# All eight cosine products of the rotary embedding on GpSimd, in a one-core vision transformer layer

## The chip, the core and the metric

The kernel runs on one core of one Trainium2 chip. The metric is the device time of one execution in microseconds (us). The core's engines are named as the profile names them: PE is TensorE (matmul; PEld its weight loads), DVE is VectorE, ACT is ScalarE, POOL is GpSimd, SP is SyncE, which here only starts transfers (DMA).

## What is computed

The input is 32 images of 256 x 256. Each goes through a wavelet tokenizer, then one transformer layer on 257 tokens (a class token and 256 rows) of width 256: a 16-head causal attention with rotary embedding, and a feed-forward part with quantised weights and activations. Cut to what matters here:

```
qkv = jnp.einsum('bsd,dhf->bshf', x, w_qkv) + b_qkv
q, k, v = jnp.split(qkv, 3, axis=-1)
q = q * cos + _rotate_half(q) * sin
k = k * cos + _rotate_half(k) * sin
scores = jnp.einsum('bhqd,bhkd->bhqk', q, k) / jnp.sqrt(jnp.float32(f)) + alibi, causal mask, softmax
h = h + einsum(attn, w_out) + b_out
h = h + ffn(layernorm(h))        # silu(gate) * up, then down; activations quantised row by row
```

## The kernel before, in words

The 32 images pass through a software pipeline of steps. A step `s` works on three images at once: part A (tokenizer and first layer norm) of image s+1, part B (the projections q, k, v and the rotary embedding) of image s, and parts C and E (attention and the feed-forward part) of image s-1. Five steps at the start and four at the end are written out; the 26 between are a loop of 13 passes over two steps. Each step has 16 slots, `k` = 0 to 15, and every engine walks the slots in the same order; what it does in a slot is fixed by tables (`QK_SLOT`, `V_SLOT`, `GU_SLOT` and others). An engine runs its own instructions strictly in order, and waits on semaphores for the others.

The rotary embedding is done in eight groups g = 0 to 7 of two 128-row blocks: groups 0 to 3 are q, groups 4 to 7 are k. They stand in slots 1, 2, 3, 4, 5, 7, 8, 9. For a group:

- PE computes the projection into `b_bank`; ACT copies it with its bias into `rq[:, g % 2]` (L501, semaphore `rq_ready`).
- SP copies `rq` to `rot[:, g % 2]` with the halves swapped, in four transfers (L392, `rot_done`). It waits for `qk_done` of group g-2, since `rot` has two halves.
- The cosine product `rq * cos` goes straight into `qt` or `kt`. It is on POOL (L475, `pcos_done`) for the groups of `COS_ON_POOL` and on DVE (L1175, `t1_done`) for the others. A q group is one instruction on 2 x 256 columns. A k group is two instructions on 2 x 128 columns, because the class token's column lies between them. The tiles `qt` and `kt` are called arena in the profile.
- POOL multiplies `rot` by the sine in place (L480, `t2_ready`) and adds it to the cosine product (L484, `qk_done`).

DVE does its cosine product in slot k of the group, POOL does all its work for the group one slot later. ACT may overwrite `rq[:, g % 2]` with group g+2 once the cosine product and the swap of group g are done (`wait_cos`). PE needs all eight groups (`qk_done`) in slot 14, for the scores of the image's first heads.

Other work that the prediction names. On DVE: `ttr` (L1055) moves scores out of PSUM with bias and row maximum; `pt_lo` (L1060, out ptr_l) makes the low half of the transposed probabilities, for which PE waits before `values`; `normalise` (L1079, out ao); the quantisation of the tokens in slot 5 (L1096 and what follows); `xn` (L1190, two instructions in slot 9), the first layer norm; `vl` (L1170), the low half of v, for which PE waits before the next v block. On POOL: the power for the second layer norm (L462, `rstd2`, in slot 5, ahead of group 3), the power for the first (L465, slot 7), and in slots 8 and 9 `hr` (L491) and `row_operators` (L446 to L455) between groups 5 and 6.

Of the kernel before, what the change touches and what calls it, by code (L numbers as in the profile page):

```python
# [40 lines left out]
WSCALE = 64.0  # L41
MAGIC = 1.5 * 2.0 ** 23
SLOTS = 16
COS_ON_POOL = [1, 3, 4, 6]
QK_GROUPS = 8


# [60 lines left out]
def vit_layer(nc, x, cls_tok, Wa, ba, Wd1, bd1, Wd2, bd2, Wd3, bd3, w_qkv, b_qkv, w_out, b_out,  # L108
              w_gate, w_up, w_down, c_cos, c_sin, c_rel, c_mask, c_row, c_avg, c_eye, out):
    with ExitStack() as ctx:  # L110
# [213 lines left out]
        def wait_cos(eng, b, g):  # L324

            on_pool = g % QK_GROUPS in COS_ON_POOL
            groups = [i for i in range(QK_GROUPS) if (i in COS_ON_POOL) == on_pool]
            done = len([i for i in groups if i <= g % QK_GROUPS]) + (len(groups) if g >= 0 else 0)
# [102 lines left out]
        def _(pool):  # L431
# [25 lines left out]
            def step(s, par):  # L457
                has_a, has_b, has_c, has_e = stages(s)
                for k in range(SLOTS):
# [8 lines left out]
                    if has_b and k - 1 in QK_SLOT:  # L468
                        g = QK_SLOT.index(k - 1)
                        if g in COS_ON_POOL:  # L470
                            pool.wait_ge(rq_ready, 8 * s + g + 1)
                            if g == COS_ON_POOL[0] and (not isinstance(s, int) or s > 1):
                                pool.wait_ge(t_done, 32 * (s - 1))
# [398 lines left out]
        def _(dve):  # L872
# [247 lines left out]
            def step(s, par):  # L1120
# [5 lines left out]
                for k in range(SLOTS):  # L1126
# [39 lines left out]
                    if has_b and k in V_SLOT:  # L1166
# [3 lines left out]
                        stt(vl[par][:, v // 2, cols], b_bank[:, :], 1.0 / WSCALE, vh[par][:, v // 2, cols], ALU.mult, ALU.subtract).then_inc(vl_done, 1)  # L1170
                    if has_b and k in QK_SLOT and QK_SLOT.index(k) not in COS_ON_POOL:
                        g = QK_SLOT.index(k)
# [98 lines left out]
```

## Time and profile before

| | before |
|---|---|
| median of 3 runs | 2415.41 us (2415.02 to 2421.36) |
| the profiled execution | 2422.74 us, span 2420.7 us |
| PE busy | 1851.4 us (76% of the span) |
| DVE busy | 1731.4 us (72%) |
| ACT busy | 1359.0 us (56%) |
| POOL busy | 1023.0 us (42%) |
| mean granted clock of PE | 0.933 of full speed |

Busy time is the sum over the whole span; no engine is busy throughout, since each waits for the others at fixed points of every step. A timeline row gives start and length in us, engine, line, what is written and read, the number of instructions, and in brackets the idle time before it and what ended that idle time.

### The profile page before, as it was taken

The numbers are of one execution on the slowest core, as the hardware profiler recorded it, in microseconds if no ns is written. First come the engines' busy times: TensorE is split into PE (matmuls) and PEld (weight loads), VectorE is DVE, ScalarE is ACT, GpSimd is POOL, SyncE is SP. The second block draws the span as 40 slices with busy tenths as digits, with TensorE's granted clock in tenths as the row PEclk, the third lists the DMA queues.
The fourth block names the chain that finished last, engine by engine and source line by source line (L and its number), as shares of the span: only waits on it lengthen the run. The fifth ranks groups of instructions, "written<-read, shape, count | busy, mean of one in ns | idle before, by whom it ended". The sixth has DMA issues, their size and how long they took to land.

```text
span 2420.7 us, 54955 instructions
## 1 busy us (share of the span) xinstructions
PE 1851.4 (76%) x16742; PEld 1334.8 (55%) x16742; DVE 1731.4 (72%) x5024; ACT 1359.0 (56%) x3841; POOL 1023.0 (42%) x1098
## 2 busy tenths in 40 slices
PE   2667878777787887777878787778778787887775
PEld 2644555555555655555556555555555555555543
DVE  2536778778777677777767776877767677777775
ACT  0125666666656565655656656665655565666653
POOL 0136445444555344445544443455534344554400
PEclk6769999999999999999999999999999999999986
DMA  7312111111111111111111111111111111111100
GB/s 180 127 35 53 40 43 49 42 42 40 42 48 49 46 41 44 42 38 40 49 50 48 39 45 40 40 39 48 49 46 41 40 42 36 47 49 45 45 10 9
DMA packets 98170, 114.79 MB, mean 47 GB/s; under 512 B 22722, under 2 KB 60067, under 8 KB 97571
## 3 DMA queue, kind: packets, MB, share of 16 engines
q1 hardware_dynamic: 97826, 110.61, 17.6%
q8 instruction: 167, 2.74, 0.5%
q14 instruction: 177, 1.44, 0.2%
HBM read 26.62 MB, written 8.42 MB: 14 GB/s over the span
## 4 chain that ended last, share of the span: by engine, by line
PE 35%; DVE 29%; issue 20%; ACT 9%; POOL 3%; SPq 2%; DVEq 1%; ACTq 0%; DMA 0%; POOLq 0%
PE bank L624 16%; PE bank L774 4%; DVE arena L1055 3%; DVE ptr_l L1060 3%; DVE arena L1207 3%; DVE es L1210 3%; DVE th L1203 3%; PE bank L858 3%; PE bank L714 2%; PE bank L712 2%; PE bank L726 2%; ACT arena L509 2%; DVE ao L1079 2%; PE bank L735 1%; PE bank L658 1%
## 5 line engine op out<-in xcount | busy, mean ns | idle before, releaser
L480 POOL TENSOR_TENSOR rot<-rot,sin 128x512 f32<-128x512 f32 x256 | 331.0, 1293 | 1072.4 <-DMA rot<-rq 1072.2
L509 ACT ACTIVATE arena<-arena,nm 128x129 f32<-128x129 f32 (+1 forms) x1024 | 458.5, 457 | 65.0 <-DVE nm L1055 65.0
L1055 DVE CUSTOM_DVE_ANT_0 arena<-bank,bias 128x129 f32<-128x129 f32 (+1 forms) x1024 | 304.9, 354 | 174.1 <-PE bank L714 164.5
L624 PE MATMUL bank<-xt_h,weights 128*128 128x256 f16 x2048 | 398.1, 282 | 20.1 <-ACT rq L501 17.6
L624 PE MATMUL bank<-arena,ptr_h 128*128 128x64 f16 x3072 | 211.1, 196 | 258.1 <-DVE ptr_l L1060 161.1
L514 ACT ACTIVATE ptr_h<-bank 128x384 f16<-128x384 f32 x512 | 249.9, 488 | 231.4 <-PE bank L726 231.3
L501 ACT ACTIVATE rq<-bank,bqk 128x256 f32<-128x256 f32 x512 | 213.8, 469 | 275.6 <-PE bank L624 270.9
L484 POOL TENSOR_TENSOR arena<-arena,rot 128x256 f32<-128x256 f32 (+1 forms) x384 | 344.4, 911 | 30.3 <-POOL rot L480 0.5
L624 PEld LDWEIGHTS bank<-arena,ptr_h 128*128 128x128 f16 x3072 | 182.1, 100 | 305.8 <-DVE ptr_l L1060 226.8
L1060 DVE TENSOR_TENSOR ptr_l<-bank,ptr_h 128x384 f16<-128x384 f32 x512 | 281.5, 550 | 53.8 <-ACT ptr_h L514 53.7
L624 PE MATMUL bank<-xt_l,weights 128*128 128x256 f16 x1024 | 288.5, 282 | 0.0
L726 PE MATMUL bank<-eye,arena 128*128 128x128 f32 x1536 | 267.3, 284 | 0.0
L624 PEld LDWEIGHTS bank<-xt_h,weights 128*128 128x128 f16 x2048 | 206.5, 101 | 88.9 <-issue 29.4
L726 PEld LDWEIGHTS bank<-eye,arena 128*128 128x128 f32 x1536 | 188.4, 146 | 65.6 <-issue 38.0
L1175 DVE TENSOR_TENSOR arena<-rq,cos 128x256 f32<-128x256 f32 (+1 forms) x192 | 132.0, 714 | 123.8 <-ACT rq L501 123.8
L624 PE MATMUL bank<-weights,xt_h 128*128 128x512 f16 x512 | 155.4, 385 | 71.1 <-DVE arena L1170 69.6
L509 ACT ACTIVATION_READ_ACCUMULATOR arena<-arena,nm 128x1 f32 x1024 | 204.7, 200 | 0.0
L624 PE MATMUL bank<-arena,ptr_l 128*128 128x64 f16 x1536 | 194.4, 196 | 0.0
L624 PE MATMUL bank<-weights,arena 128*128 128x256 f16 x1536 | 179.0, 273 | 2.8 <-DVE arena L1060 2.6
L475 POOL TENSOR_TENSOR arena<-rq,cos 128x256 f32<-128x256 f32 (+1 forms) x192 | 178.2, 942 | 0.0
L714 PE MATMUL bank<-arena 64*128 64x257 f32 x1024 | 161.1, 392 | 0.0
L624 PEld LDWEIGHTS bank<-weights,arena 128*128 128x128 f16 x1536 | 149.4, 98 | 20.7 <-DVE arena L1060 3.1
(187 smaller groups left out, 3562.1 us busy)
## 6 DMA issues: line engine op xcount, KB each, us to landing
rot<-rq SPq DMA_DIRECT2D x1024, 64.0 KB, 2.0
arena<-in_x SPq DMA_DIRECT2D x4, 2048.0 KB, 18.2
xin<-in_x SPq DMA_DIRECT2D x32, 256.0 KB, 2.7
hr<-hr SPq DMA_DIRECT2D x32, 256.0 KB, 2.4
out<-h SPq DMA_DIRECT2D x64, 128.0 KB, 1.7
arena<-in_L_attn_w_qkv SPq DMA_DIRECT2D x2, 1536.0 KB, 6.5
arena<-in_L_attn_w_out SPq DMA_DIRECT2D x1, 1024.0 KB, 10.1
arena<-in_L_ffn_w_gate SPq DMA_DIRECT2D x1, 1024.0 KB, 6.4
```

What stands on the lines that cost most here:

```text
L475: ins = pool.tensor_tensor(dst, rq[:, g % 2, :, cols], cos[:, cols].unsqueeze(1).broadcast_to([P, 2, cols.stop - cols.start]), ALU.mult)
L480: pool.tensor_tensor(r, r, sin[:, :].unsqueeze(1).broadcast_to([P, 2, SIDE]), ALU.mult).then_inc(t2_ready, 1)
L484: ins = pool.tensor_tensor(dst, dst, rot[:, g % 2, :, cols], ALU.add)
L501: return act.activation(dst, src, ACT.Identity, **kw)
L509: act.activation(cols, cols, ACT.Exp, bias=nm[:, t, h:h + 1], scale=-1.0, accum_out=rs[:, t, h:h + 1]).then_inc(e_done, 1)
L514: act.activation(dst, src, ACT.Copy).then_inc(hi_done, 1)
L624: ins = pe.matmul(dst, lhs[l], rhs[r], start=start and n == 0, stop=stop and n == len(parts) - 1)
L714: pe.matmul(bank[:, W0:SCOLS], qt[par][half, j, P:SIDE], kt[par][half, j, :], start=True, stop=True).then_inc(s_ready, 1)
L726: ins = pe.transpose(pt_bank[use % 2][:, n * P:(n + 1) * P], r[:, col:col + P], eye[:, :])
L1055: dve.tensor_tensor_reduce(r[:, cols], bank[:, cols], b, -1.0, 3.0e38, ALU.add, ALU.min, nm[:, t, h:h + 1]).then_inc(t_done, 1)
L1060: tt(dst, src, hi, ALU.subtract).then_inc(pt_free, 1)
L1175: ins = tt(dst, rq[:, g % 2, :, r], cos[:, r].unsqueeze(1).broadcast_to([P, 2, r.stop - r.start]), ALU.mult)
```

## The change

The table that names the groups whose cosine product is on POOL now holds all eight.

```diff
-COS_ON_POOL = [1, 3, 4, 6]
+COS_ON_POOL = list(range(8))
```

The code that reads the table stays as it is. DVE's branch is never taken, and `wait_cos` always waits on `pcos_done`. The wait on `t_done` that keeps POOL's first cosine product of an image from overwriting a `qt` still in use is now ahead of group 0 instead of group 1.

On DVE, in a written-out step, at the end of slot 8 and in slot 9 (`es` are scales of the quantisation, `ptr_l` the low probabilities, `xn` the first layer norm, `arena<-rq,cos` the cosine product):

```order
 L1117 TENSOR_SCALAR es<-es,wsc 128x1 [waits chain_e]
 L1118 TENSOR_SCALAR es<-es 128x1
-L1175 TENSOR_TENSOR arena<-rq,cos 128x2x128 [waits rq_ready]
-L1175 TENSOR_TENSOR arena<-rq,cos 128x2x128
 L1060 TENSOR_TENSOR ptr_l<-bank,ptr_h 128x384 [waits hi_done]
 L1190 TENSOR_SCALAR xn<-hh,mv,rstd 128x256 [waits rstd_ready]
```

Group 7's two instructions are gone from between the scales and the low probabilities; groups 0, 2 and 5 go in the same way from slots 1, 3 and 7.

On POOL, from the start of an image to the power of the second layer norm, before:

```order
L480 TENSOR_TENSOR rot<-rot,sin 128x512 [waits rot_done0]
L484 TENSOR_TENSOR arena<-arena,rot 128x512 [waits t2_ready,t1_done]
L475 TENSOR_TENSOR arena<-rq,cos 128x512 [waits t_done,rq_ready]
L480 TENSOR_TENSOR rot<-rot,sin 128x512 [waits rot_done1]
L484 TENSOR_TENSOR arena<-arena,rot 128x512 [waits t2_ready,pcos_done]
L480 TENSOR_TENSOR rot<-rot,sin 128x512 [waits rot_done0]
L484 TENSOR_TENSOR arena<-arena,rot 128x512 [waits t2_ready,t1_done]
L462 TENSOR_TENSOR rstd<-ve,negh 128x2 [waits var2_ready]
```

and the same place with the change:

```order
L475 TENSOR_TENSOR arena<-rq,cos 128x512 [waits t_done,rq_ready]
L480 TENSOR_TENSOR rot<-rot,sin 128x512 [waits rot_done0]
L484 TENSOR_TENSOR arena<-arena,rot 128x512 [waits t2_ready,pcos_done]
L475 TENSOR_TENSOR arena<-rq,cos 128x512 [waits rq_ready]
L480 TENSOR_TENSOR rot<-rot,sin 128x512 [waits rot_done1]
L484 TENSOR_TENSOR arena<-arena,rot 128x512 [waits t2_ready,pcos_done]
L475 TENSOR_TENSOR arena<-rq,cos 128x512 [waits rq_ready]
L480 TENSOR_TENSOR rot<-rot,sin 128x512 [waits rot_done0]
L484 TENSOR_TENSOR arena<-arena,rot 128x512 [waits t2_ready,pcos_done]
L462 TENSOR_TENSOR rstd<-ve,negh 128x2 [waits var2_ready]
```

A cosine product (L475) now stands ahead of the sine product of group 0, and another ahead of that of group 2. In the same way one of two instructions comes ahead of group 5 (after the power L465) and one ahead of group 7 (the last of the image).

## Rows read from the trace of the kernel before

**Rows 1.** PE's waits from 200 to 2300 us: total us, times, longest us

```profile
PE bank L624 <- DVE ptr_l L1060: 154.3, 92, 4.2
PE bank L624 <- DVE arena L1170: 63.0, 58, 1.8
```

**Rows 2.** Groups by line and shape, 500 to 2000 us: busy us, mean ns, idle before

```profile
L475 POOL TENSOR_TENSOR arena<-rq,cos 128x256 f32<-128x256 f32 x86 | 63.5, 759 | 0.0
L475 POOL TENSOR_TENSOR arena<-rq,cos 128x512 f32<-128x512 f32 x43 | 57.3, 1333 | 0.0
L1175 DVE TENSOR_TENSOR arena<-rq,cos 128x256 f32<-128x256 f32 x86 | 45.8, 573 | 41.0 <-ACT rq L501 41.0
L1175 DVE TENSOR_TENSOR arena<-rq,cos 128x512 f32<-128x512 f32 x44 | 45.7, 1038 | 34.4 <-ACT rq L501 34.4
```

**Rows 3.** Timeline of DVE around the cosine products of groups 0, 2 and 5

```profile
1016.50 0.68 DVE L1175 TENSOR_TENSOR arena<-rq,cos 128x512 f32<-128x512 f32 x1
...
1018.23 0.29 DVE L1055 CUSTOM_DVE_ANT_0 arena<-bank,bias 128x129 f32<-128x129 f32 x1 [0.58 <-PE bank L714]
...
1024.83 1.67 DVE L1175 TENSOR_TENSOR arena<-rq,cos 128x512 f32<-128x512 f32 x1 [1.01 <-ACT rq L501]
...
1028.70 0.29 DVE L1055 CUSTOM_DVE_ANT_0 arena<-bank,bias 128x129 f32<-128x129 f32 x1 [1.74 <-PE bank L714]
...
1044.91 0.76 DVE L1175 TENSOR_TENSOR arena<-rq,cos 128x256 f32<-128x256 f32 x2 [2.04 <-ACT rq L501]
...
1046.74 0.69 DVE L1203 SCALAR_TENSOR_TENSOR th<-th,bank 128x512 f32<-128x512 f32 x1 [0.60 <-ACT th L591]
```

**Rows 4.** Timeline of DVE at group 7, in two consecutive steps

```profile
1054.90 1.05 DVE L1175 TENSOR_TENSOR arena<-rq,cos 128x256 f32<-128x256 f32 x2
1055.87 0.55 DVE L1060 TENSOR_TENSOR ptr_l<-bank,ptr_h 128x384 f16<-128x384 f32 x1
1056.34 1.13 DVE L1190 TENSOR_SCALAR xn<-hh,mv,rstd 128x256 f32<-128x256 f32 x2
...
1127.06 1.83 DVE L1175 TENSOR_TENSOR arena<-rq,cos 128x256 f32<-128x256 f32 x2
```

**Rows 5.** Timeline of PE in the first of these steps, after group 7

```profile
1056.47 0.23 PE L624 MATMUL bank<-arena,ptr_h 128*128 128x64 f16 x2 [1.44 <-DVE ptr_l L1060]
...
1059.85 0.61 PE L624 MATMUL bank<-weights,xt_h 128*128 128x512 f16 x2 [1.64 <-DVE arena L1170]
```

**Rows 6.** Timeline of POOL in the first of these steps

```profile
1020.88 1.27 POOL L480 TENSOR_TENSOR rot<-rot,sin 128x512 f32<-128x512 f32 x1 [24.83 <-DMA rot<-rq]
...
1029.44 1.28 POOL L480 TENSOR_TENSOR rot<-rot,sin 128x512 f32<-128x512 f32 x1 [1.83 <-DMA rot<-rq]
...
1048.96 1.27 POOL L480 TENSOR_TENSOR rot<-rot,sin 128x512 f32<-128x512 f32 x1 [5.94 <-DMA rot<-rq]
...
1055.63 1.69 POOL L475 TENSOR_TENSOR arena<-rq,cos 128x256 f32<-128x256 f32 x2
...
1061.71 1.28 POOL L484 TENSOR_TENSOR arena<-arena,rot 128x256 f32<-128x256 f32 x2
```

**Rows 7.** Timeline of POOL at group 2 and the power, one step before rows 6

```profile
960.40 1.26 POOL L484 TENSOR_TENSOR arena<-arena,rot 128x512 f32<-128x512 f32 x1
961.63 1.27 POOL L480 TENSOR_TENSOR rot<-rot,sin 128x512 f32<-128x512 f32 x1
...
964.36 0.69 POOL L462 TENSOR_TENSOR rstd<-ve,negh 128x2 f32<-128x2 f32 x1
```

**Rows 8.** Timeline of DVE where it takes that power

```profile
965.61 1.15 DVE L1096 TENSOR_SCALAR th<-h,mv,rstd 128x256 f32<-128x256 f32 x2
```

**Rows 9.** Timeline of PE: slot 14, and the same place in the first step

```profile
1068.55 0.49 PE L712 MATMUL bank<-arena 64*128 64x129 f32 x4
...
196.03 0.51 PE L712 MATMUL bank<-arena 64*128 64x129 f32 x4 [1.93 <-POOL arena L484]
```

**Rows 10.** Windows over a loop end: PE, PEld, DVE, ACT, POOL busy, PEclk

```profile
1080.00:1087.00 7.00, 5.09 (x31) 3.71 (x32) 2.87 (x12) 1.36 (x5) 0.00 (x0) 0.53 0.07 23
```

## The prediction

> **What bounds the kernel now.** I read the page first: no engine is busy throughout, PE 76% of the span, DVE 72%, POOL 42%. So the time is set by waits between engines, and the second view is that of the waits. PE's largest are on DVE: 154.3 us on the low half of the probabilities and 63.0 us on the low half of v [rows 1]. DVE's work therefore counts where PE waits behind it, and only there. The third view is the timeline of two consecutive steps in the loop, engine by engine, read around each cosine product. A step takes some 70 us: 2420.7 us of span over 34 steps.
>
> **What is removed from DVE.** Six instructions per image. Their price is not their busy time: it depends on what DVE meets behind them.
>
> - Group 0: DVE does it at 1016.50 in 0.68 us, and a little later stands idle 0.58 us for PE's scores. Group 2: 1.67 us from 1024.83, and then 1.74 us idle for the next scores. Group 5: 0.76 us from 1044.91, and then 0.60 us idle for ACT's tanh. [rows 3] In all three DVE runs into a later wait that it doesn't set, and in the timeline of PE I found no wait on DVE between. With these products gone DVE waits longer there. Worth: 0.
> - Group 7: DVE is late here. It does not stand idle before the product (no bracket), goes at once to the low probabilities at 1055.87, and PE, which has waited 1.44 us for them, starts at 1056.47 [rows 4, 5]. Then come the layer norm, the next scores and the low half of v, for which PE waits 1.64 us [rows 5]. What is taken away here moves everything behind it earlier.
>
> The size: in this step the product holds DVE for 0.97 us (1054.90 to 1055.87), in the next for 1.83 less an overlap of 0.08, so 1.75 us [rows 4]. The mean over the loop comes from the grouped rows: the 128x256 instructions are 573 ns on average [rows 2], half of them group 5's pairs. Those take 0.76 us a pair with the same overlap of 0.08, so 0.42 us each, and group 7's are then 2 x 0.573 - 0.42 = 0.73 us each, a pair 2 x 0.73 - 0.08 = 1.38 us and 1.30 us to the start of what follows. Times 31 images (image 0 has no attention beside it): **-40 us**.
>
> Why 0.73 where the same instruction takes 0.42 in group 5? POOL is at work at the same time. The product reads two SBUF tensors, as POOL does, and the lengths fit one waiting for the other: in group 2 the 128x512 product takes 1.67 us, and 0.68 where POOL is idle [rows 3]. The Trainium skill (SBUF — State Buffer, "SBUF: two separate sides") says that DVE, in a two-port mode or with two SBUF inputs, and POOL lock a shared pair of ports for a whole instruction. By that rule, the trace agrees, the group 7 product goes but the next DVE instruction of that kind inherits the lock.
>
> **What that costs back.** The layer norm (two instructions, 1.13 us together from 1056.34 [rows 4]) ends at 1057.47, just when POOL's cosine product of group 6 is over (1055.63 + 1.69 = 1057.32 [rows 6]). It is held up by POOL already. If it comes 0.97 us earlier, it meets the same POOL instructions at another place. In this step I expect the first half of POOL's pair to end it, so that 0.2 us of the 0.97 are not gained; in the other step, where POOL is earlier than DVE, nothing is lost. Bounds: it could still end at 1057.47 (loss 0.97 per image, gain 0) or be held up not at all (its share of the wait is about 0.5 us, as a gain). I take 0.1 us for each image: **+3 us**.
>
> **What is added on POOL.** Per image two instructions of 128x512 (1.27 us unhindered, 1.33 mean) and four of 128x256 (0.76 mean) [rows 2], 5.7 us. Place by place:
>
> - Group 0: POOL stands idle 24.83 us until the swapped copy lands [rows 6]. `rq` is ready over 4 us before that: DVE's own product of it starts at 1016.50, POOL's sine product at 1020.88 [rows 3, 6]. Hidden. The wait on `t_done` that goes with it has long been met: those scores were finished in the step before.
> - Group 5: 5.94 us idle before its sine product [rows 6], and `rq` is ready by 1044.91, when DVE takes it, 4.0 us ahead of the sine product at 1048.96 [rows 3, 6]. The pair (1.4 us) is hidden, and `row_operators` behind it does not move.
> - Group 2: in the step shown POOL stands idle 1.83 us [rows 6], enough for 1.27. In the step before it goes from 960.40's addition straight to the sine product at 961.63 [rows 7], and so it is in 12 of 32 images, of which this one stands for all. There the product delays sine, addition and the power L462 by up to 1.27. The power ends at 965.05 and DVE takes it at 965.61 [rows 7, 8], so 0.56 us are free. Where POOL's product of group 1 was held up by DVE's of group 2 (the mean is 1.33 against 1.27 unhindered [rows 2], so it is not often), part comes back. Late by 1.27 - 0.56 = 0.7 at most; I take 0.3; behind it are DVE's quantisation, ACT's rounding and PE's transposes, which PE waits for. 12 x 0.3: **+4 us**. Bounds: 0, and 12 x 0.7 = 8.
> - Group 7: no idle time before it, as POOL comes from `row_operators`. Its pair adds 1.4 us to the end of the image on POOL. The last addition ends at 1062.99 (1061.71 + 1.28 [rows 6]), and PE's scores that need it start at 1068.55 [rows 9]: 5.56 us free. Less 1.4, and less 1.3 that PE comes earlier, 2.9 remain. Hidden.
> - The first step has no attention to hide behind: PE waits 1.93 us for POOL's last addition [rows 9], and starts with it. There the products of groups 2 and 7 both count, 1.3 and 1.4: **+3 us**.
>
> ACT's permission to overwrite `rq` now always comes from POOL, one or two groups ahead: group 5's pair is over at 1044.91 + 1.4 = 1046.3, and ACT copies group 7 more than 4 us later, group 2's is over before its sine product at 1029.44. No new wait.
>
> **The sum**: -40 + 3 + 4 + 3 = -30 us. The profiled execution took 2422.74, 7.3 us more than the median of the runs, and would be 2393; on the median, 2415.41 - 30 = **2385 us**. By the bounds alone: from 0 to -31 x (1.30 + 0.5) = -56.
>
> **The rivals.**
>
> 1. No change. The layer norm ends where it did, because POOL's instructions decide it, and the gain of group 7 becomes a longer L1190. For it: 1057.32 and 1057.47 lie so close. Against it: PE's wait on the low probabilities ends ahead of the layer norm and shrinks anyway, and POOL's pair leaves a gap between its halves. Time: 2415 - 0 to 5, so 2410 to 2415.
>
> 2. Slower, because POOL brings the second layer norm's power late in every image. It decides once the power ends more than 0.56 + 1.30 = 1.9 us later than now. That takes both products of groups 0 and 2 in the open, 2.5 us with nothing hidden, for instance if the swapped copies landed earlier than I read. Then (2.5 - 0.56 - 1.30) x 31 = 20 us: 2435. Against it: 24.83 us of idle time ahead of group 0. The Trainium skill (GPSIMD Engine Reference, "Engine selection") advises against two-input elementwise work on GpSimd, as about twice as slow as on VectorE. The trace agrees on the ratio, 1.27 against 0.68 us. If all of POOL's work were in the open, as that rule takes it, the rows give 31 x (5.7 - 1.3) = 136 us more: 2550; nothing in POOL's idle time supports that, 1 in 100.
>
> 3. A larger gain, from PE's clock. Around a loop end it falls: 0.53 from 1080 to 1087, where PE was busy 5.09 of 7 us at near half speed [rows 10]. Such a stretch follows idle time of PE, and the change takes idle time away. If half of the 13 loop ends lost 4 us of it, that is 26 us more, with the lock's upper bound 2340 to 2360. It can also fall the other way, with clocks lower at other places by chance, 10 us.
>
> **How the numbers follow.** The forecast (2360 to 2408) has 0.62, the larger gain 0.16, no change 0.13, slower 0.09. A measurement can tell 0.3% here, 7 us. Faster is 0.62 + 0.16 = 0.78, same 0.13, slower 0.09. The range reaches down to 2350, by the two upper bounds together in part (0.06 below), and up to 2412 into the no-change case (about 0.12 above).
>
> **What would show it.** L1175 is gone from DVE and POOL's L475 stands at 384 instructions, busy about 1200 us, 50%. The idle time of DVE on ACT's `rq` (41.0 and 34.4 us [rows 2]) reappears as longer waits on PE's scores (L1055) and the tanh. PE's wait on the low probabilities falls by about 1.3 us per image. POOL's idle time before L480 shrinks by some 4 us per image. The period of a pass falls by 2 to 2.5 us. Wrong would be: L1190's pairs well over 1.13 us with the same period (rival 1), PE or DVE waiting for L462 or L484 (rival 2), or a different share of slow clock (rival 3).

## The result and the profile after

The changed kernel takes 2393.16 us (median of 4 runs, 2381.5 to 2394.61). Before beside it took 2415.02, 2415.41 and 2421.36 us. Two slow runs of before, 4532.66 us here and 5400.2 us beside the experiments, are left out of all ratios. By the two medians that is 22 us less. The ratio is 0.9877, with a 95% interval of 0.9849 to 0.9906, which is 30 us less (23 to 37). The profiled executions went from 2422.74 to 2394.61 us, 28 us less. The forecast was 2385, 30 less.

Part 1 of the page of the changed kernel: busy time, share of the span, instructions.

```profile
PE 1850.9 (77%) x16742; PEld 1336.2 (56%) x16742; DVE 1617.7 (68%) x4832; ACT 1356.1 (57%) x3841; POOL 1175.2 (49%) x1290
```

DVE has 114 us less to do, POOL 152 us more, and the span is shorter by 28: most of the work that was taken from DVE was not in anyone's way. Which part was, the waits of PE show, 200 to 2300 us (total us, times, longest us):

```profile
PE bank L624 <- DVE ptr_l L1060: 110.2, 93, 4.3
PE bank L624 <- DVE ao L1079: 100.4, 90, 2.7
PE bank L624 <- DVE arena L1170: 66.9, 57, 2.3
```

The wait on the low probabilities fell from 154.3 to 110.2 us [rows 1], 44 us or 1.4 for each of 31 images. Not all of it is gain: the wait for `ao` was 88.2 us before and is 12 us longer now, that for the low half of v 4 us longer. 44 - 12 - 4 = 28 us is what the span lost; the other waits of PE changed by 3.3 us or less each.

The same step as in [rows 4], DVE's timeline in the changed kernel:

```profile
1046.38 0.20 DVE L1118 TENSOR_SCALAR es<-es 128x1 f32<-128x1 f32 x1
1046.51 0.55 DVE L1060 TENSOR_TENSOR ptr_l<-bank,ptr_h 128x384 f16<-128x384 f32 x1
1046.97 0.81 DVE L1190 TENSOR_SCALAR xn<-hh,mv,rstd 128x256 f32<-128x256 f32 x2
1047.70 0.28 DVE L1055 CUSTOM_DVE_ANT_0 arena<-bank,bias 128x129 f32<-128x129 f32 x1
...
1048.81 1.10 DVE L1140 TENSOR_SCALAR q<-arena 128x1024 f16<-128x1024 f32 x1
1049.84 0.68 DVE L1170 SCALAR_TENSOR_TENSOR arena<-bank,arena 128x512 f16<-128x512 f32 x1
```

and PE's, with its waits in brackets:

```profile
1047.11 0.23 PE L624 MATMUL bank<-arena,ptr_h 128*128 128x64 f16 x2 [0.47 <-DVE ptr_l L1060]
...
1050.57 0.60 PE L624 MATMUL bank<-weights,xt_h 128*128 128x512 f16 x2 [1.73 <-DVE arena L1170]
```

The low probabilities stand right behind the scales. PE waits 0.47 us for them where it waited 1.44 [rows 5]: 0.97 less, just what the product had held DVE. The wait for the low half of v stays (1.64 before, 1.73 now), since PE itself is there earlier. The layer norm L1190 is shorter than before, and L1140 behind it longer. The timeline of POOL beside them has the reason. One of its instructions, L480, is itself longer (1.71 us) than an unhindered one (1.27):

```profile
1045.82 1.26 POOL L450 TENSOR_TENSOR rowop<-op_now,avg 128x512 f32<-128x512 f32 x1
1047.05 0.58 POOL L453 TENSOR_TENSOR s<-s 128x128 f32<-128x128 f32 x1
...
1047.96 1.41 POOL L475 TENSOR_TENSOR arena<-rq,cos 128x256 f32<-128x256 f32 x2
1049.33 1.71 POOL L480 TENSOR_TENSOR rot<-rot,sin 128x512 f32<-128x512 f32 x1
```

L1190 now meets the tail of `row_operators`. L1140 meets the second half of group 6's cosine product, and the sine product L480 behind that is held up by L1140 in turn. Over the loop, in the groups by line and shape, 500 to 2000 us (busy us, mean ns, idle before), first before and then the changed kernel:

```profile
L1140 DVE TENSOR_SCALAR q<-arena 128x1024 f16<-128x1024 f32 x44 | 30.3, 688 | 0.0
L1190 DVE TENSOR_SCALAR xn<-hh,mv,rstd 128x256 f32<-128x256 f32 x44 | 27.6, 668 | 0.0
```

```profile
L475 POOL TENSOR_TENSOR arena<-rq,cos 128x256 f32<-128x256 f32 x176 | 124.8, 730 | 41.9 <-ACT rq L501 41.9
L475 POOL TENSOR_TENSOR arena<-rq,cos 128x512 f32<-128x512 f32 x88 | 111.5, 1268 | 434.2 <-ACT rq L501 434.2
L1140 DVE TENSOR_SCALAR q<-arena 128x1024 f16<-128x1024 f32 x44 | 38.8, 881 | 0.0
L1190 DVE TENSOR_SCALAR xn<-hh,mv,rstd 128x256 f32<-128x256 f32 x44 | 19.9, 494 | 0.0
```

Two of each line to a step: L1190 gives back 2 x 0.174 = 0.35 us, L1140 takes 2 x 0.193 = 0.39.

**Where in the step the time went.** I took the start of every DVE instruction against the start of L1164 (slot 15) in 29 steps of each trace, and the mean over them. The difference to before, in us:

```
place in the step                after   7 alone, again
slot 0, first scores (L1055)     -0.03       -0.17
slot 0, their second half        +0.24       -0.18
slot 8, end of scales (L1118)    +0.34       +0.11
slot 9, ptr_l (L1060)            -0.91       -1.14
slot 9, next scores (L1055)      -1.28       -1.48
slot 9, v (L1170)                -0.92       -1.15
slot 15, next step (L1164)       -1.02       -1.41
```

The whole gain is made between the scales and `ptr_l` (1.25 us), as forecast. But 0.34 us of it has been lost earlier in the step. A jump of 0.27 us stands at one place in slot 0 (from -0.03 to +0.24), ahead of all groups; from there to the scales the value moves between +0.10 (slot 2) and +0.34.

### The profile page after: what moved, and what is told of

Same layout as the page of the kernel before. It is cut to its first block, busy times and chain, and to the rows that moved or that the text cites. A ratio compares the mean times of both kernels' runs of the same rounds, so it can differ in the third digit from the quotient of the medians.

```text
span 2392.8 us, 55176 instructions
## 1 busy us (share of the span) xinstructions
PE 1850.9 (77%) x16742; PEld 1336.2 (56%) x16742; DVE 1617.7 (68%) x4832; ACT 1356.1 (57%) x3841; POOL 1175.2 (49%) x1290
## 4 chain that ended last, share of the span: by engine, by line
PE 33%; DVE 33%; issue 18%; ACT 10%; POOL 2%; SPq 2%; DVEq 1%; ACTq 0%; DMA 0%; POOLq 0%
PE bank L624 15%; DVE arena L1207 4%; DVE arena L1055 4%; DVE es L1210 4%; DVE th L1203 3%; PE bank L858 3%; DVE ptr_l L1060 3%; PE bank L774 3%; PE bank L714 2%; ACT arena L509 2%; PE bank L712 2%; PE bank L726 2%; DVE arena L1170 2%; DVE ao L1079 1%; ACT q2t L543 1%
## 5 line engine op out<-in xcount | busy, mean ns | idle before, releaser
L475 POOL TENSOR_TENSOR arena<-rq,cos 128x256 f32<-128x256 f32 (+1 forms) x384 | 344.8, 912 | 652.8 <-ACT rq L501 652.8
L480 POOL TENSOR_TENSOR rot<-rot,sin 128x512 f32<-128x512 f32 x256 | 335.8, 1312 | 239.6 <-DMA rot<-rq 239.4
L484 POOL TENSOR_TENSOR arena<-arena,rot 128x256 f32<-128x256 f32 (+1 forms) x384 | 332.3, 880 | 37.3 <-POOL rot L480 0.9
L624 PE MATMUL bank<-weights,xt_h 128*128 128x512 f16 x512 | 155.1, 385 | 72.7 <-DVE arena L1170 71.1
L712 PE MATMUL bank<-arena 64*128 64x129 f32 x1024 | 130.8, 333 | 39.6 <-issue 35.1
```

What stands on the lines that cost most here:

```text
L475: ins = pool.tensor_tensor(dst, rq[:, g % 2, :, cols], cos[:, cols].unsqueeze(1).broadcast_to([P, 2, cols.stop - cols.start]), ALU.mult)
L480: pool.tensor_tensor(r, r, sin[:, :].unsqueeze(1).broadcast_to([P, 2, SIDE]), ALU.mult).then_inc(t2_ready, 1)
L484: ins = pool.tensor_tensor(dst, dst, rot[:, g % 2, :, cols], ALU.add)
L624: ins = pe.matmul(dst, lhs[l], rhs[r], start=start and n == 0, stop=stop and n == len(parts) - 1)
L712: pe.matmul(bank[:, 0:W0], qt[par][half, j, 0:P], kt[par][half, j, 0:W0], start=True, stop=True)
```

## The experiments

The clock has to be read with each. The mean granted clock of a whole run is 0.91 to 0.95 of full speed, and it differs between runs of one kernel. Over 135 runs of all kernels here, each against the mean of its own kernel and chip, 0.01 more clock goes with 15.6 us less time (standard error 0.9). This is a relation between runs; that the clock is the cause is shown only where an experiment below moves it. "At 0.936" below is a kernel's median, moved by this slope to the median clock of before (0.935 to 0.937).

### Group 7 alone, and all but group 7

```diff
-COS_ON_POOL = [1, 3, 4, 6]
+COS_ON_POOL = [1, 3, 4, 6, 7]              # first kernel
+COS_ON_POOL = [0, 1, 2, 3, 4, 5, 6]        # second kernel
```

> Only the cosine product of group 7 moves to GpSimd; groups 0, 2 and 5 stay on VectorE. Theory (group 7 is the one that pays, by its own 1.3 us and by a shorter first layer norm): all of the gain, 22 to 32 us, a time of 2387 to 2396. Rival (the gain comes from VectorE's load as a whole, spread over the four groups): a quarter of it, 5 to 8 us, 2410 to 2413.

> Groups 0, 2 and 5 move to GpSimd and group 7 stays on VectorE. Theory: no gain, within 5 us of 2418, since VectorE runs into later waits behind each. Rival (spread over the groups): three quarters of the gain, about 19 us, 2399. If GpSimd's product of group 2 delays the power of the second layer norm, some us slower than before.

Group 7 alone: 2380.07 us, ratio 0.9844 [0.9782, 0.9906], clock 0.9365. All but group 7: 2432.39 us, ratio 1.0056 [1.0025, 1.0087], clock 0.9315. So group 7 is the whole gain, and more than the 22 to 32 us that were expected. The other three give nothing: without it they cost 10 us by the medians and 14 by the ratio, 7 of them by the clock. The Trainium skill (Perfetto Trace Analysis, "Optimizing Scalar/DVE Operations") warns that offloading between VectorE and GpSimd might not help, since they share a port. For three of the four products the trace agrees; for the fourth, ahead of PE's wait, it does not. Group 7 alone also isolates group 5's pair on DVE, and all but 7 isolates group 7's (groups by shape, 500 to 2000 us, one fence for each kernel):

```profile
L1175 DVE TENSOR_TENSOR arena<-rq,cos 128x256 f32<-128x256 f32 x44 | 16.7, 421 | 37.4 <-ACT rq L501 37.4
```

```profile
L1175 DVE TENSOR_TENSOR arena<-rq,cos 128x256 f32<-128x256 f32 x44 | 24.8, 604 | 0.0
```

Group 5's takes 0.42 us an instruction, as the prediction worked out; group 7's is over 0.6 in both kernels.

### POOL's row operators moved away from group 7

```diff
-SUMS_SLOT = 9
+SUMS_SLOT = 12
```

once in the kernel before, once in the changed one.

> The kernel before, with GpSimd's row operators moved from slot 9 to slot 12, behind the rotary work, where GpSimd is idle; nothing else. If VectorE's cosine product of group 7 and the first layer norm are held up by GpSimd's instructions at that place (the row operators and the product of group 6), the pair of group 7 falls from 1.38 towards 0.76 us and the layer norm from 1.3 towards 0.8, and the step shortens by up to 1 us: 2388 to 2400. Rival (the lengths are VectorE's own, or other GpSimd instructions take the place of the moved ones): no change, 2415 to 2420.

> All eight products on GpSimd and the row operators in slot 12. With the products gone from VectorE only the layer norm (0.85 us now, 0.73 at best) is left to be held up there: within 6 us of the changed kernel's 2393, if anything faster. Rival (GpSimd's end of the image matters): over 10 us faster, since its last addition then comes some 4 us earlier.

Before with this edit: 2471.62 us, ratio 1.0212 [1.0144, 1.028], clock 0.916. Changed kernel with it: 2423.27 us, ratio 1.0004 [0.9972, 1.0037], clock 0.9255; 30 us above the changed kernel. Both expectations were wrong. DVE in a step of the former:

```profile
1073.70 1.66 DVE L1175 TENSOR_TENSOR arena<-rq,cos 128x256 f32<-128x256 f32 x2
1075.28 0.55 DVE L1060 TENSOR_TENSOR ptr_l<-bank,ptr_h 128x384 f16<-128x384 f32 x1
1075.75 1.67 DVE L1190 TENSOR_SCALAR xn<-hh,mv,rstd 128x256 f32<-128x256 f32 x2
```

and POOL beside it:

```profile
1072.94 1.26 POOL L480 TENSOR_TENSOR rot<-rot,sin 128x512 f32<-128x512 f32 x1
1074.35 1.55 POOL L484 TENSOR_TENSOR arena<-arena,rot 128x256 f32<-128x256 f32 x2
1075.86 1.41 POOL L480 TENSOR_TENSOR rot<-rot,sin 128x512 f32<-128x512 f32 x1
```

Now both the product (1.66 us) and the layer norm (1.67) are held up, each until an instruction of the rotation is over. In before they took 1.05 and 1.13 us in the first step of [rows 4], and the layer norm's instructions were 668 ns in the mean against 796 here. What DVE meets there decides, not how busy POOL is. Measured as in the table above, the step of before grows by 1.62 us with this edit. 0.84 of it arises between the scales and the next scores, by these hold-ups, and 0.3 at slot 15, where PE's clock is low more often (in the whole trace 412 us at 1.2 GHz against 329). The rest is spread over the step and was not taken apart. The Trainium skill (SBUF — State Buffer, "SBUF: two separate sides") says that whichever of the two starts first holds the shared pair for a whole instruction. The trace agrees in both directions: L1190 here ends 0.15 us behind POOL's L480, and in the changed kernel's step above L480 took 1.71 us with L1140 ahead of it. L1190 has one SBUF tensor as input, so that by the rule it would have to be in a two-port mode, which no view shows.

### PE kept at work in slot 14

```diff
+                for again in range(4 if h == 14 else 1):
                     for n, col in enumerate((0, W0, W0 + P + 1)):
                         ins = pe.transpose(pt_bank[use % 2][:, n * P:(n + 1) * P], r[:, col:col + P], eye[:, :])
```

The three transposes of head 14 are issued four times, to the same result. It was done in before and in the changed kernel.

> The kernel before, with the three transposes of head 14 (slot 14) issued four times over with the same data to the same bank: 9 more short matmuls in a place where TensorE waits 2 us for the low probabilities. The result is the same. If idle time there is what lets TensorE's clock fall at the end of a step, clock and time improve: by up to 1.4 us in each step that had a fall there, 10 to 30 us in all. Rival (TensorE is the bound there, or the falls come from elsewhere, as at the loop's end): the same time or up to 30 us slower.

> The same repeated transposes in the changed kernel. In its written-out steps the 1.5 us won in slots 8 to 12 are lost again where TensorE runs slots 14 and 15 at half clock. Theory (the clock's fall eats part of the gain): those steps shorten from 65.0 to about 63.6 us, and the kernel by 10 to 40 us from 2393. Rival (slot 14 takes the won time back whatever the clock is): written-out steps stay at 65.0 us, no gain.

In before: 2389.2 us, ratio 0.9882 [0.9851, 0.9912], clock 0.945. Nine more matmuls in each step, for nothing, make it 31 us faster by the medians, 29 by the ratio. Windows over the 11 us ahead of slot 15 at the same loop end (columns as in [rows 10]), before and then with the edit:

```profile
1066.00:1077.00 11.00, 8.75 (x77) 6.55 (x75) 9.16 (x27) 7.47 (x22) 0.00 (x0) 0.85 0.04 14
```

```profile
1051.00:1062.00 11.00, 9.49 (x101) 6.99 (x99) 9.56 (x30) 8.04 (x23) 0.00 (x0) 1.00 0.01 2
```

The granted clock rises from 0.85 to 1.00 of full speed there, so the stretches at the lower level, 1.2 GHz, are gone. In the whole trace PE is at 1.2 GHz for 329 us before and 261 us with the edit. The difference is 68 us, and 68 us of it had lain in slots 14 and 15 of 29 steps, where none is left. At half the clock that is worth up to 34 us; the spans differ by 35. The step shows the place: with the edit it is 0.1 us shorter up to slot 14 and 1.02 at slot 15, so that 0.93 of it, 27 us over 29 steps, is won between the two.

In the changed kernel the edit brings 2388.34 us, ratio 0.9871 [0.9843, 0.99], clock 0.939: 2 to 5 us less than without it, inside the intervals. The first two of its complete steps, which are written out, take 63.5 and 64.6 us where they took 65.0 and 65.2, so that the theory holds for the first of them; the 10 to 40 us for the kernel did not come. In the trace there is no low clock left in slots 14 and 15, and 63 us less of it in all. But this execution (2374.94 us) is the fastest of five, the others being 2387 to 2392, so that it can't stand for the median. Why the median gains so little stays open.

### Group 7 with each of the others

```diff
+COS_ON_POOL = [1, 3, 4, 6, 7]              # again
+COS_ON_POOL = [0, 1, 3, 4, 6, 7]           # and 0
+COS_ON_POOL = [1, 2, 3, 4, 6, 7]           # and 2
+COS_ON_POOL = [1, 3, 4, 5, 6, 7]           # and 5
```

> The same kernel as in the run with group 7 alone, on the chip of the three that follow, as their measure: 0.984 of before, 2380 us, is expected again by every theory. In its 26 loop steps the first two instructions of the scores' copy (L1055, slot 0) stood 0.22 us apart, in the full change 0.47.

> Groups 7 and 0 moved. Theory A (fixed gaps: in the loop's steps DVE shows extra gaps of 0.2 to 0.4 us at places that shift when instructions are taken out of its stream, and that is what groups 0, 2 and 5 cost): some gap moves onto the path, 0.2 us x 26 = 5 us above group 7 alone, 2385. Theory B (POOL's lateness at group 2 brings the power L462 late): group 0 is hidden behind 24 us of idle time, so as group 7 alone, 2380, and the waits for L462 stay at 3.7 us in total. Theory C (PE's clock differs by chance between kernels): a time that goes with the granted clock, about 15 us for each 0.01 of it, whichever group is moved.

> Groups 7 and 2 moved. Theory A: as with group 0, 2385, with gaps at other places. Theory B: this is the group that costs, 2388 to 2392, with DVE's L1096 waiting or held up more in slot 5 (0.2 us a step more between its first and what follows). Theory C: goes with the clock alone.

> Groups 7 and 5 moved. Theory A: 0.2 to 0.4 us in half of the loop's steps in slot 7, 3 to 5 us, 2384. Theory B: nothing, 2380. Theory C: goes with the clock alone.

> The changed kernel once more, beside before: 0.988 of it, 2393 us, by every theory; with group 7 alone 0.984. If it comes out at 0.984 the difference between the two was chance.

| on POOL beside 1, 3, 4, 6 | us | ratio | clock | at 0.936 |
|---|---|---|---|---|
| 7, again | 2382.57 | 0.9858 [0.9826, 0.9889] | 0.936 | 2383 |
| 7, 0 | 2384.26 | 0.9867 [0.9835, 0.9898] | 0.9355 | 2383 |
| 7, 2 | 2386.75 | 0.9865 [0.9836, 0.9893] | 0.9345 | 2384 |
| 7, 5 | 2413.19 | 0.9967 [0.9944, 0.9991] | 0.927 | 2399 |
| 7, 0, 2, 5, again | 2392.79 | 0.9886 [0.9855, 0.9918] | 0.9345 | 2390 |

Group 0 and group 2 cost nothing that can be told: 2 to 4 us by the medians, inside the intervals. The times alone would leave room for my +4. But theory B's path (the power L462 comes late) is not there: DVE waits 3.8 us for L462 with 7 and 2, 4.6 with 7 alone. Group 5 costs 31 us when it is moved with 7 alone, and no theory had that. By the slope 14 of the 31 are clock (theory C). The trace (2420.82 us, the slowest of the 12 runs) has 9 of the other 17 as hold-ups at the old place; what the remaining 8 are was not found. DVE and POOL in a step of it:

```profile
1131.09 1.52 DVE L1190 TENSOR_SCALAR xn<-hh,mv,rstd 128x256 f32<-128x256 f32 x2
...
1133.64 1.10 DVE L1140 TENSOR_SCALAR q<-arena 128x1024 f16<-128x1024 f32 x1
```

```profile
1130.77 1.27 POOL L450 TENSOR_TENSOR rowop<-op_now,avg 128x512 f32<-128x512 f32 x1
...
1132.78 1.41 POOL L475 TENSOR_TENSOR arena<-rq,cos 128x256 f32<-128x256 f32 x2
```

L1190 has come while POOL's L450 runs to 1132.0 and takes 1.52 us; in the changed kernel's step above L450 was over at 1047.1, next to the layer norm's start, and the pair took 0.81. The offset between the two engines tells it throughout: group 6's product (L475) starts 1.69 us behind L1190 in the step of 1.52 us, and 0.99 behind it in that of 0.81. With 7 and 5 it starts 1.49 us behind or later in 17 of 29 steps, with 7 alone in one. The mean pair is 1.26 us against 0.94: 0.32 x 29 = 9 us. So the pair of group 5 did push POOL's work behind it back, which I had called hidden. It has no fixed price. Against 7 alone, L450 starts 0.56 us later in the step with 7 and 5 and L1190 only 0.13; with 0 and 2 moved too, L450 is 0.28 later and L1190 0.23. So there the offset is 0.81 in the mean (0.75 with 7 alone, 1.17 with 7 and 5) and the pair 0.91.

The full change stands above group 7 alone by 13 us in the first pair of measurements (ratios 0.9877 and 0.9844) and by 10 in the second (0.9886 and 0.9858). By the ratios it is 8 and 7 us; in the second pair the two kernels ran on different chips, each beside before. The intervals overlap both times, so that this is likely and not shown. The traces have a possible cause for part of it, a gap in DVE's own stream. In slot 0, changed kernel, then group 7 alone:

```profile
398.32 0.29 DVE L1055 CUSTOM_DVE_ANT_0 arena<-bank,bias 128x129 f32<-128x129 f32 x1 [1.27 <-PE bank L714]
398.72 0.08 DVE L1055 DVE_READ_ACCUMULATOR2_ANT nm<- 128x1 f32 x1
398.79 0.43 DVE L1055 CUSTOM_DVE_ANT_0 arena<-bank,bias 128x257 f32<-128x257 f32 x1
```

```profile
397.02 0.29 DVE L1055 CUSTOM_DVE_ANT_0 arena<-bank,bias 128x129 f32<-128x129 f32 x1 [1.28 <-PE bank L714]
397.24 0.08 DVE L1055 DVE_READ_ACCUMULATOR2_ANT nm<- 128x1 f32 x1
397.24 0.42 DVE L1055 CUSTOM_DVE_ANT_0 arena<-bank,bias 128x257 f32<-128x257 f32 x1
```

The two score instructions start 0.47 us apart instead of 0.22, and no other engine is waited for. It is so in all 26 steps of the loop and in none of the written-out ones: 26 x 0.25 = 6.5 us. The gap stands at the same place in all four traces that have all eight products on POOL, the experiments with the row operators and the transposes among them. PE waits for `ao`, which comes behind the scores with three instructions between, and this is the wait that grew by 12 us (88.2 to 100.4; 98.2 in the second trace, 86.8 with 7 alone). With 7 and 0, 7 and 2, or 7 and 5 there is no gap at this place. The gap is not the only way to a longer wait, though: all but 7 has none there, and 95.6 us for `ao`. Nor does all of the gap last: behind it the changed kernel is 0.42 us later in the step than 7 alone, in slot 6 only 0.08, at the end of the scales 0.23. That the time depends on the gap is argued from these figures; no run has the full change without it. Theory A is thus half right: the gap is real and its place depends on the stream, but it came with none of the groups singly.

### Both gains together

```diff
-COS_ON_POOL = [1, 3, 4, 6]
+COS_ON_POOL = [1, 3, 4, 6, 7]
+                for again in range(4 if h == 14 else 1):
```

> Group 7 alone on POOL and the repeated transposes of head 14, which leave the output as it is. If the two gains are separate they add: 0.984 x 0.988 = 0.972, 2355 us. If group 7's gain already uses the higher clock (as with the full change, where the transposes brought 5 us of the 31 that they brought before): 2370 to 2378, and the granted clock at 0.94 as without them.

2370.77 us (2365.68 to 2375.86), ratio 0.9802 [0.9779, 0.9824], clock 0.938: the fastest of all kernels here, 22 us below the changed kernel. The time is in the range of the second expectation; its reason is borne out only in part. Of the 31 us that the transposes bring in before, 12 are left with group 7 moved (2382.57 to 2370.77). The low clock in slots 14 and 15 is gone here as well (54 us in 29 steps with 7 alone, 68 in before), so group 7's gain had used up only a small part of it. But the 20 us of each step ahead of them hold more of it: 41 us, against 14 with 7 alone. In the whole trace 286 us are left of 310. Half of these 24, the price of running at half the clock, is about the 12 us of the gain.

## Why the prediction was right, point by point

- **Group 7, -40.** Right. L1118 to `ptr_l` is 1.25 us shorter in each step (1.30 was taken). Group 7 alone gives 34 to 38 us by its two ratios. The sharing of 573 ns between the pairs was right as well: 422 ns for group 5's instructions and 701 for group 7's in the trace of before.
- **Groups 0, 2 and 5 worth 0 on DVE.** Right in that nothing is gained: all but 7 is no faster than before. DVE's waits grew in their place, though not where I said. From 200 to 2300 us, changed kernel:

```profile
DVE arena L1055 <- PE bank L714: 199.8, 93, 5.4
DVE ptr_l L1060 <- ACT ptr_h L514: 186.0, 141, 3.3
```

  I named the scores and the tanh. The scores took 45 us (155.1 before) and the tanh 9 (18.5, now 27.6), and 137 us went to the wait for ACT's high half of the probabilities (48.9 before), which stands nearer behind groups 0 and 2.
- **Layer norm, +3.** The size was small and of the wrong sign at its place: L1190 became shorter by 0.35 us a step, since in its new place it meets the short row operators. Then L1140, which the prediction did not name, took 0.39. The sum, +0.04 a step, is nearly what was put down (0.1), but by a path that I had not seen.
- **The power L462, +4.** Not there. DVE waits for it 3.0 us in all, 2.6 in before, and 7 with 2 costs nothing that can be told.
- **ACT's copies, no new wait.** Wrong. ACT waits for POOL's cosine product before it may overwrite `rq`, in the changed kernel from 200 to 2300 us:

```profile
ACT rq L501 <- POOL arena L475: 11.7, 4, 4.0
```

  In before it is once, 1.9 us, and so with 7 alone and with 7 and 0. All but 7 has the same 11.7 us, and 7 and 2 has 19.5 us in six waits. So the wait comes with group 2. In the times it can't be told from nothing.
- **First steps, +3.** Right in the number, in part by luck: the first complete step begins at 265.0 instead of 262.3 us, 2.7 later. PE's wait for POOL's last addition grew from 1.9 to 4.1 us. It is 3.8 with 7 alone and 3.8 with 7 and 2 as well, so that group 7 accounts for most of it and group 2 for none that can be seen, where 1.3 was put down. And the start of this step varies more than that: 266.1 in the second trace of the changed kernel, 255.9 to 264.1 in the other kernels here.
- **Additions on POOL hidden.** Right in so far as no wait for L484 is among PE's large ones. But that `row_operators` does not move behind group 5's pair was wrong: L450 starts 0.56 us later in the step with 7 and 5 than with 7 alone. It cost there, though no engine waits for POOL: by where POOL holds up DVE.
- **Not in the sum:** the gap in slot 0 (6.5 us, if all of it lasts), and the clock. In the profiled pair the low clock is equal in all (329 and 329 us), so the 28 us as a whole are no clock. It lies elsewhere, though: 133 instead of 150 us in the 29 steps, and as much more outside them, so that up to half of these 17 us, 9 of the steps' 29.6, may be clock. And rival 3's mechanism lives, with the other sign. A written-out step shows it. In before it has no low clock and lasts 65.1 us (262.35 to 327.49). In the changed kernel it lasts 65.0 (265.04 to 330.01), though DVE's stretch from L1203 ahead of the scales (298.39, now 301.02) to L1109 in slot 14 (326.36, now 327.43) is 1.56 us shorter. PE's timeline of its end:

```profile
324.78 0.23 PE L624 MATMUL bank<-arena,ptr_h 128*128 128x64 f16 x2 [2.08 <-DVE ptr_l L1060]
...
325.52 1.87 PE L858 MATMUL bank<-wdn,q2t 128*128 128x256 f16 x8
327.19 1.06 PE L865 MATMUL bank<-eye,q 128*128 128x128 f16 x8
328.04 1.06 PE L764 MATMUL bank<-eye,xn 128*128 128x128 f32 x4
```

  against before:

```profile
324.46 1.04 PE L858 MATMUL bank<-wdn,q2t 128*128 128x256 f16 x8
325.53 0.61 PE L865 MATMUL bank<-eye,q 128*128 128x128 f16 x8
325.97 0.61 PE L764 MATMUL bank<-eye,xn 128*128 128x128 f32 x4
```

  Behind a wait of 2.08 us the same matmuls take 1.87, 1.06 and 1.06 us, not 1.04, 0.61 and 0.61, and ACT and DVE wait for them. In the loop such dips were there already, and the gain survives.
- **Sum.** 29 steps x 1.02 = 29.6, less 2.7, is 27; the spans differ by 27.9. A pass of the loop is 2.1 us shorter (2 to 2.5 forecast). The mechanism of the -40 was right. That the total came so near is in part luck: 10 us of cost were put down for the layer norm, the power and the first steps, of which the first two cost about 1. What took their place is 0.34 us a step lost ahead of the scales, 10 us, for which the sum had no term; how much of that is the gap in slot 0 is not shown.
- **The rest of its working.** The prediction gives its range as 2360 to 2408 and again as 2350 to 2412; the time lies in both. It divides by 34 steps where there are 5 + 26 + 4 = 35, which changes nothing. POOL's idle time before L480 fell by much more than 4 us an image (768 to 170 us, from 500 to 2000 us), but 476 us of idle time stand before L475 instead, so that POOL's wait has moved ahead of the cosine product rather than gone.

Open: what makes the gap in slot 0, why the repeated transposes bring so little in the changed kernel, and why low clock gathers ahead of slot 14 in some orders (7 and 5, row operators later) and not in others. No run here took them apart.

## What to carry to other kernels

Price a moved instruction by what stands behind it: three of four products here were worth nothing, and the one in front of a wait of PE was worth at least as much as all four together. When VectorE and GpSimd both read SBUF, look at which instruction each meets after the move: an offset of 1.69 instead of 0.99 us between them nearly doubled a layer norm (1.52 for 0.81 us). And compare the granted clock before believing a difference of under 1%: nine matmuls without a use, in the right slot, were worth as much in the kernel before (31 us) as the change itself.

## What I had not expected of the hardware

- Useless matmuls pay, in the kernel before. Nine transposes of 128x128 a step raised the mean granted clock from 0.937 to 0.945 and took 31 us off (1.2%).
- One kernel's runs differ by up to 31 us (2415.46 to 2446.29 for all but 7), and the clock (0.944 and 0.926) accounts for 28 of it by the slope of 15.6 us per 0.01.
- GpSimd's instructions lengthen a VectorE instruction with one SBUF tensor and per-partition scalars as well: L1140 from 688 to 881 ns in the mean, L1190 between 0.73 and 1.67 us a pair.
- Gaps of 0.25 us in VectorE's stream, in the loop's steps alone, move when instructions elsewhere in the loop are taken out (slot 0 of the changed kernel has one, slot 0 with 7 alone has none).
